# Value matmuls of six groups in f32r high and low parts, in a two-layer attention kernel

## What is computed

```python
def _L0_conv_ref(x, ...):            # layer 0, 64 inner channels
    g_x     = einsum('ic,bcn->bni', g_w, xf) + g_b
    theta_x = einsum('ic,bcn->bni', theta_w, xf) + theta_b
    phi_x   = einsum('ic,bcn->bin', phi_w, xf) + phi_b
    f = softmax(einsum('bni,bim->bnm', theta_x, phi_x), axis=-1)
    y = einsum('bnm,bmi->bni', f, g_x)
    return einsum('ci,bin->bcn', W_w, y.transpose(0, 2, 1)) + W_b + xf

def _L1_conv_ref(x, ...):            # layer 1, 128 channels
    q = einsum('oc,bcn->bno', Wq, xf) + bq
    k = einsum('oc,bcn->bcn', Wk, xf) + bk   # row sums of Wk scale x
    v = einsum('oc,bcn->bno', Wv, xf) + bv
    attn = softmax(einsum('bnc,bcm->bnm', q, k) / sqrt(128), axis=-1)
    return x + einsum('bnm,bmc->bnc', attn, v).transpose(0, 2, 1)
```

## Time and profile before

| | |
|---|---|
| median of 3 runs | 3556.16 us |
| profiled execution, its own time | 3554.52 us |
| its span | 3552.7 us |
| TensorE granted clock, mean | 0.992 |
| busy: TensorE / its weight loads | 98% / 56% |
| busy: DVE / ACT / POOL | 66% / 42% / 70% |
| one block of layer 1, from the second on | 62.1 us |

### The profile page before, as it was taken

The page is one execution under the profiler, slowest core; times in us unless marked ns, Lnnn a source line. Parts: engine busy times, 40 slices in busy tenths (PEclk is TensorE's granted clock), DMA queues, the critical chain, the costliest instruction groups (busy, mean ns, idle before and its releaser), DMA issues.

```text
span 3552.7 us, 45057 instructions
## 1 busy us (share of the span) xinstructions
PE 3476.9 (98%) x12740; PEld 1999.6 (56%) x12740; DVE 2360.3 (66%) x3029; ACT 1494.4 (42%) x2017; POOL 2500.8 (70%) x1142
## 2 busy tenths in 40 slices
PE   7999999999999999999999999999999999999999
PEld 4445466666555446666655455666665544566665
DVE  4555577777655557777765555777776555677775
ACT  4445433333444543333345454333334445333333
POOL 4888666666788866666678886666668888566665
PEclk9999999999999999999999999999999999999999
DMA  1000000000000000000000000000000000000000
GB/s 42 19 12 18 27 10 22 12 21 15 19 17 17 18 23 15 16 18 18 13 19 18 18 16 22 16 15 21 15 19 13 18 18 16 18 13 14 13 7 15
DMA packets 34032, 61.66 MB, mean 17 GB/s; under 512 B 5280, under 2 KB 5920, under 8 KB 33568
## 3 DMA queue, kind: packets, MB, share of 16 engines
q1 hardware_dynamic: 33824, 59.23, 5.5%
HBM read 42.44 MB, written 16.78 MB: 17 GB/s over the span
## 4 chain that ended last, share of the span: by engine, by line
PE 90%; DVE 5%; issue 3%; ACT 1%; POOL 0%; SPq 0%; DVEq 0%; DMA 0%; ACTq 0%
PE acc_out L432 22%; PE acc_out L429 14%; PE rough L385 13%; PE scores L407 9%; PE scores L410 7%; PE scores L412 6%; PE scores L416 6%; PE scores L413 6%; DVE piece_max L730 2%; DVE rparts L757 2%; PE rough L367 2%; PE acc_out L373 1%; PE acc_out L452 1%; PE acc_out L441 1%; PE acc_out L447 1%
## 5 line engine op out<-in xcount | busy, mean ns | idle before, releaser
L271 POOL TENSOR_TENSOR sums<-sums,probs 128x1024 f32<-128x1024 f32 x886 | 2117.8, 2390 | 706.2 <-ACT probs L648 566.0
L730 DVE TENSOR_REDUCE piece_max<-rough 128x1 f32<-128x512 f32 x2024 | 1309.5, 684 | 645.1 <-PE rough L385 644.7
L648 ACT ACTIVATE probs<-probs 128x1024 f32<-128x1024 f32 x512 | 542.0, 1059 | 1220.7 <-DVE probs L747 1218.0
L432 PE MATMUL acc_out<-probs,v_vals 128*128 128x512 f32 x2048 | 963.4, 593 | 0.0
L747 DVE TENSOR_TENSOR probs<-scores,shift_rows 128x1024 f32<-128x1024 f32 x512 | 625.4, 1221 | 462.3 <-PE scores L416 448.6
L655 ACT ACTIVATE probs<-scores 128x1024 f32<-128x1024 f32 x512 | 524.5, 1024 | 692.2 <-PE scores L410 690.3
L429 PE MATMUL acc_out<-probs,g_vals 128*64 128x512 f32 x2048 | 549.7, 617 | 0.0
L432 PEld LDWEIGHTS acc_out<-probs,v_vals 128*128 128x128 f32 x2048 | 384.2, 189 | 285.7 <-issue 247.2
L412 PE MATMUL scores<-qry_a,k_hi 128*128 128x512 f32 x1024 | 532.9, 520 | 0.0
L407 PE MATMUL scores<-qry_a,phi_a 128*128 128x512 f32 x1024 | 449.4, 439 | 0.0
L410 PE MATMUL scores<-qry_b,phi_b 128*128 128x512 f32 x1024 | 404.5, 395 | 0.0
(11 more groups left out here) (86 smaller groups left out, 2117.2 us busy)
## 6 DMA issues: line engine op xcount, KB each, us to landing
x_q<-x SPq DMA_DIRECT2D x32, 256.0 KB, 2.7
x_res<-x SPq DMA_DIRECT2D x32, 256.0 KB, 3.0
mid<-mid_new SPq DMA_DIRECT2D x32, 256.0 KB, 2.2
x_q<-mid SPq DMA_DIRECT2D x32, 256.0 KB, 2.8
x_res<-mid SPq DMA_DIRECT2D x32, 256.0 KB, 3.2
out<-result SPq DMA_DIRECT2D x32, 256.0 KB, 2.3
x_kv<-x SPq DMA_DIRECT2D x24, 256.0 KB, 2.8
probs<-x SPq DMA_DIRECT2D x2, 1024.0 KB, 6.5
```

Source lines behind the costliest of these rows:

```text
L271: eng.tensor_tensor(sums[:, parity], sums[:, parity], probs[:, s % P_BUFS], ALU.add).then_inc(s_plus, 1)
L432: last = mm(acc_out[:, parity], cols(v_vals, tile, KT), p, start=tile == 0, stop=tile == TILES - 1)
L648: nc.scalar.activation(probs[:, s % P_BUFS], probs[:, s % P_BUFS], ACT.Exp, scale=SCALES[1]).then_inc(s_whole, 1)
L730: nc.vector.reduce_max(piece_max[:, t, c:c + 1], src, AX.X).then_inc(s_reduced, 1)
```

## The change

In layer 1, the groups 1, 3, 5, 9, 11 and 13 of each block are "halved": their values and probabilities are each split into an f32r high part and a low part, and the value group is six f32r matmuls (high x high, high x low, low x high, for two tiles) instead of two f32 matmuls. The product of the two low parts is left out. For that

- ACT computes the exponential of such a group twice: first into p_hi (f32r), then in place as before; it also copies half of each value block into v_hi.
- POOL subtracts: p_lo = probs - p_hi (128 x 1024) in step s, ahead of the add of the same group; v_lo = v_vals - v_hi (128 x 256) at s = 14 of layer 0's blocks and in the turn.
- TensorE waits for p_lo and v_lo before such a value group; the other ten groups stay as they were.

```diff
+V_LO_AT = 14
+HALVED = (1, 3, 5, 9, 11, 13)
...
+        v_hi = sb("v_hi", [P, BLOCKS, TPG * KT], F32R)
+        v_lo = sb("v_lo", [P, BLOCKS, TPG * KT], F32R)
+        p_hi = sb("p_hi", [P, 2, GC], F32R)
+        p_lo = sb("p_lo", [P, 2, GC], F32R)
...
+            def halved_values(b, g, nth, parity, s):
+
+                pe.wait_ge(s_p_lo, halved(nth, s))
+                pe.wait_ge(l_v, (b + 1) * BLOCKS)
+                n = HALVED.index(s) % 2
+                for h in range(TPG):
+                    hi = v_hi[:, s // TPG, h * KT:(h + 1) * KT]
+                    lo = v_lo[:, s // TPG, h * KT:(h + 1) * KT]
+                    at = slice(h * QB, (h + 1) * QB)
+                    mm(acc_out[:, parity], hi, p_hi[:, n, at], start=False, stop=False)
+                    mm(acc_out[:, parity], hi, p_lo[:, n, at], start=False, stop=False)
+                    last = mm(acc_out[:, parity], lo, p_hi[:, n, at], start=False, stop=False)
+                last.then_inc(s_used, 1)
...
-                    if s >= LAG:
+                    if s >= LAG and st.layer == 1 and s - LAG in HALVED:
+                        halved_values(st.b, st.g, st.nth, st.parity, s - LAG)
+                    elif s >= LAG:
                         value_group(st.layer, st.g, st.parity, s - LAG)
+                    elif st.prev == 1 and GROUPS + s - LAG in HALVED:
+                        halved_values(st.b if st.layer == 1 else st.b - 1, st.g - 1,
+                                      st.nth - 1, 1 - st.parity, GROUPS + s - LAG)
...
             def take_v(n, c, src):
                 act.wait_ge(p_v, n + 1)
+                copy(v_hi[:, bass.ds(c, 1)] if not isinstance(c, int) else v_hi[:, c:c + 1],
+                     src[:, TPG * KT:].unsqueeze(1))
                 copy(cols(v_vals, c), src).then_inc(h_v, 1)
...
-            def probs_shifted(nth, s):
+            def probs_shifted(g, nth, s):
 
                 act.wait_ge(s_shifted, shifted(nth, s))
+                if s in HALVED:
+                    n = HALVED.index(s)
+                    act.wait_ge(s_used, g * GROUPS + HALVED[n - 2] + 1 + P_BUFS - (GROUPS if n < 2 else 0))
+                    nc.scalar.activation(p_hi[:, n % 2], probs[:, s % P_BUFS], ACT.Exp, scale=SCALES[1])
                 nc.scalar.activation(probs[:, s % P_BUFS], probs[:, s % P_BUFS], ACT.Exp,
                                      scale=SCALES[1]).then_inc(s_whole, 1)
...
+            def split_v(n, c):
+                pool.wait_ge(h_v, n + 1)
+                at = bass.ds(c, 1) if not isinstance(c, int) else slice(c, c + 1)
+                lo_part(v_lo[:, at], cols(v_vals, 2 * c + 1, TPG * KT).unsqueeze(1), v_hi[:, at], l_v)
+
+            def split_probs(g, nth, s):
+                n = HALVED.index(s) % 2
+                pool.wait_ge(s_whole, whole_of(g, s))
+                lo_part(p_lo[:, n], probs[:, s % P_BUFS], p_hi[:, n], s_p_lo)
...
             def block_program(st):
                 for s in range(GROUPS):
+                    if st.layer == 1 and s in HALVED:
+                        split_probs(st.g, st.nth, s)
                     if s < GROUPS - 2 or not st.ends:
                         add(pool, st.layer, st.g, st.parity, s)
...
+                    if s == V_LO_AT and st.kv:
+                        split_v(st.nth - 1, st.i - 1)
```

More of the change, by code:

```diff
@@ L167, in build @@
         s_k_hi = sem("s_k_hi")
-        p_v, h_v = sem("p_v"), sem("h_v")
+        p_v, h_v, l_v = sem("p_v"), sem("h_v"), sem("l_v")
+        s_p_lo = sem("s_p_lo")
         s_settled = {nc.gpsimd: sem("s_settled_pool"), nc.sync: sem("s_settled_sp")}
@@ L272, in add, with halved @@
                               ALU.add).then_inc(s_plus, 1)
+        def halved(nth, s):
+            return nth * len(HALVED) + HALVED.index(s) + 1
         def before(st):
@@ L556, in block_program @@
                     for s in range(GROUPS - LAG, GROUPS):
-                        value_group(st.layer, st.g, st.parity, s)
+                        if st.layer == 1 and s in HALVED:
+                            halved_values(st.b, st.g, st.nth, st.parity, s)
+                        else:
+                            value_group(st.layer, st.g, st.parity, s)
                     if st.turn:
@@ L687, in block_program @@
                     if st.layer == 1:
-                        probs_shifted(st.nth, s)
+                        probs_shifted(st.g, st.nth, s)
                     if s in (DEN_AT + 1, DEN_AT + 2) and st.prev is not None:
@@ L887, in turn @@
                 split_k(nth, BLOCKS - 1)
+                split_v(nth, BLOCKS - 1)
             run_all(pool, turn, block_program)
```

## The result

The changed kernel takes 3496.6 us (median of four runs, 3495.22 to 3498.05), the kernel before 3555.93 in the same comparison. The ratio is 0.9836, with a 95% interval of 0.9823 to 0.9848: 1.6% faster. The forecast was 3495 within 3488 to 3502. The profiled execution took 3498.05 us (span 3496.2), 56.5 less than that of before; the sum had said 61.2.

A forecast was written before the change was run, and what follows sets the result against it. TensorE's instruction stream, busy 98%, was taken as the bound. Savings of 56.4 + 4.2 + 1.05 - 0.5, 61 us, gave 3493.3 for the profiled run, 3495 as median; own range 3488 to 3502, full range 3488 to 3551.

The forecast's parts named there:

- the sum: Whole kernel: 27 steady blocks x (1.56 + 0.53) = 56.4, plus 4.2 and 1.05, less 0.5: 61 us off.
- The value groups: TensorE, layer 1: each halved value group goes from 1.73 to 1.38 us, saving 0.35.
- Which of the six count: Steady layer 1 block: of six short value groups five count, 5 x 0.35 - 0.04 - 0.15 = 1.56 us.
- the third piece of step 12: TensorE's third rough piece in step 12 waits for DVE's reduction, so the short value group's 0.35 us is lost.
- saved TensorE time alone (67 us): 192 short value groups, 0.35 us each: 67 us in all if TensorE alone decides.
- The 0.53 us stop: Step 7, steady layer 1 block: TensorE's second rough piece waits for DVE's reduction; the change gains this 0.53 us.
- margin of 0.11 us: At the reciprocals, DVE reaches line 757 at 16.32 us after group 1's shift starts, 0.11 before POOL's fourth add.
- rival (a): At the reciprocals DVE misses the gap between POOL's adds; steady block gains 0.09 us, total 7, 3549; chance 0.21.
- the subtraction wait for add 4: DVE's second small reciprocal operation (line 759) waits for POOL's fourth add until 18.85, taking about 2.4 us.
- about 46.5: Very last block: POOL's 13 adds, 6 splits and fold take about 46.5 us, making the end 0.5 us longer.
- (b): Rival: some blocks catch DVE's gap at the reciprocals and some miss it, as jitter decides: 3505 to 3540; chance 0.10.
- (c): Rival: POOL becomes the bound if a 1024-wide split costs over 3.4 us; 3726 at 4.8; chance 0.06 with another rival.

The follow-up runs named there:

- run 3: The changed kernel with group 9 not halved (five halved groups): 3495.40 us, ratio to before 0.9831.
- run 4: The changed kernel with the last third rough piece of layer 1 in step 13 instead of 12: 3485.52 us, ratio to before 0.9803.
- run 5: The kernel before, with POOL's low part of the next queries in step 7 instead of 5 in layer 1 blocks: 3546.24 us, ratio 0.9975.
- run 1: The changed kernel with all layer 1 value groups back as two f32 matmuls, splits still made but unused: 3582.32 us, ratio to before 1.0076.
- run 2: The changed kernel without POOL's 192 subtractions, the p_lo matmul using p_hi again: 3491.45 us, ratio to before 0.9820.
- run 8: The changed kernel with the last third piece in step 13 and no group halved in the very last block: 3483.47 us, ratio to before 0.9800.
- run 7: The changed kernel with group 7 halved too and layer 1's third pieces in steps 7, 8, 11, 13: 3487.00 us, ratio to before 0.9809.

## Why the prediction was right

**The value groups.** Six f32r matmuls 0.230 apart, 1.38 us: as in the rows above. TensorE waited for p_lo only in the last block, and for v_lo nowhere.

**Which of the six count.** Group 9 was said to be lost to the third piece of step 12. Runs 3 and 4 show it from both sides: its short form gave nothing, and 11 us came at once when the piece left that step. Counting saved TensorE time alone (67 us) would have been 8 us too much, and is no farther off only because this loss (31 x 0.35 = 11) and the gain below (run 5: 9) nearly cancel.

**The 0.53 us stop.** It went, and run 5 shows that it was what the prediction said. Run 1 shows the other side: the same splits with DVE 0.35 us later cost 27 us. The step of the prediction that gave the sign of this term worked with a margin of 0.11 us between line 757 and add 4. In the block above the cast is issued at 16.26 in that count (575.35 less 559.09, the start of group 1's shift) where 16.32 was worked out, and add 4 starts at 16.55 where 16.43 was. Both errors, 0.06 and 0.12, fell to the safe side, and together they are larger than the margin. Over the 26 steady blocks that passed, the cast starts 0.05 to 0.29 us ahead of add 4. So the mechanism was right, and that it came out on this side was in part luck; the prediction itself gave rival (a) 0.21.

**A detail that was wrong.** I had the subtraction wait for add 4 (2.4 us). In most blocks of the first three images it too slips through, in 0.16; in others it takes 2.27 to 2.36. What decides is which comes first: in the first sort the subtraction starts 0.01 to 0.02 us ahead of add 4, in the second 0.06 to 0.16 behind it. The two sorts of blocks are equally long:

```profile
575.35 0.23 DVE L797 CAST rparts<-rcol 128x4 fp32r<-128x4 f32 x1
635.49 0.17 DVE L797 CAST rparts<-rcol 128x4 fp32r<-128x4 f32 x1
695.42 0.23 DVE L797 CAST rparts<-rcol 128x4 fp32r<-128x4 f32 x1
```

The subtraction behind the middle one took 2.27 us, behind the others 0.16. They are 60.1 and 59.9 us apart, and it is the second stretch that has the long wait in it. So one wait is hidden in DVE's slack and two are not, which is why the cast decides and the subtraction does not.

**The sum, place by place.** From the cast in one image's first steady block to the next image's it is 877.6 us before (515.8 to 1393.4) and 861.3 after (515.42 to 1376.68): 16.4 saved, where the terms give 7 x 2.09 + 1.05 + 0.35 = 16.0; the next two images save 16.7 and 15.2. Layer 0's blocks are as long as before (46.3). The last image saves 7.9 (399.1 to 391.2) where the terms give about 12, and that is 4.1 of the 4.7 us between the sum and the profiled run. Another 1.2 stand ahead of the very first cast (113.69 against 112.46, in layer 0), which the traces of all ten kernels place anywhere from 112.1 to 113.7; the rest nearly cancels. Three places hold the 4.1. Between the second and third cast stands a halt of DVE that the kernel before has too, but here TensorE's clock fell after it (below): 62.1 us against 62.0, nothing saved. Then comes a block of rival (a), the only one among the 27:

```profile
3217.35 1.51 DVE L797 CAST rparts<-rcol 128x4 fp32r<-128x4 f32 x1
3218.89 2.31 DVE L799 TENSOR_TENSOR rparts<-rcol,rparts 128x4 fp32r<-128x4 f32 x1
```

It lasts 59.6 us where its neighbours last 58.2. And the last block was mis-sized. From the shift of its group 1 to the last cast it takes 55.4 us (3432.84 to 3488.23), 1.7 more than before (53.7, 3491.01 to 3544.68), where the terms of the prediction give 0.9 in this count (0.5 with the 0.35 saved ahead of it). The path was right: POOL's row, then DVE's adds and fold. But the row takes 47.2 us where "about 46.5" was put. TensorE's wait for p_lo is not what decides: run 1 makes the same splits and nobody waits for them, and its last block takes 55.2 us in the same count (3517.49 to 3572.70), with DVE's last adds waiting for POOL there too. With five splits (run 3) it is 53.2 (3430.99 to 3484.20). Run 2 prices POOL's splits in the end at 3.6 us, and run 8 prices halving the last block at 1.7 by its trace.

**The rivals.** (a) was a real state of this kernel, one block in 27, and run 1 is it throughout; (b), a mixture, is strictly what happened, though at 1 in 27, and not by jitter: it is the block in which DVE had halted, and the same block has a long cast in runs 3, 4, 7 and 8 too (1.42 to 2.27 us). (c) did not come: a 128x1024 split into f32r took 2.39 us, an add 2.41, as the equal prices at 512 had said. But its mechanism, POOL as the bound, did show in the last block, and POOL's lateness cost TensorE time in run 7.

## What to carry to other kernels

When one engine is full, price a change by where its shorter instruction stands: ahead of a wait that another engine sets, it is worth nothing, and moving the wait by a step (one number of a table) was worth 11 us beside the 59 of the whole change here. Two SBUF operations on 2 KB each can cost microseconds if they come while another engine holds the port; look up in a timeline on which instruction they land before and after the change, since work added to the other engine can move them into a seam as well as out of it. And where a step is repeated 27 times with the same phase, a third of a microsecond in the arrival of one engine (run 1: 27 us) is not noise that averages out but a cliff.

## What the runs showed of the hardware

- A small DVE operation can pass between two POOL instructions that follow each other without a pause: 0.23 us at 575.35 and 0.16 at 575.62, while one add runs from 573.16 for 2.40 us and the next starts at 575.64. The Trainium skill (SBUF — State Buffer, Who interferes with whom) has the one that starts first hold the shared port pair for its whole instruction; the traces agree (2.26 and 2.27 in run 1), and show that a small operation issued up to 0.02 us ahead of the next POOL instruction still passes, while one issued 0.06 behind its start waits for all of it.
- DVE's waiting time is inside its instruction durations, so its busy time fell by 5 us a block with the same instructions. A busy share of such an engine is not its load. ACT shows no such waiting here: its 128x1024 exponentials out of SBUF took 1.04 to 1.07 us each, before and after.
- At the start of a block of the last image (3196.68) DVE had stood 4.56 us with nothing to wait for that the profile shows ("issue"), and TensorE stood behind it until 3198.5. In the stretch 3198 to 3204 (last row) the mean granted clock was 0.72, so TensorE ran part of it at the lower level, 1.2 GHz, and its four value records printed 3.44 us instead of 1.88. The kernel before has a like halt at the same place (4.40, to 3248.66), but its clock stayed at 1.00; TensorE stood idle for 1.02 us there and for 1.56 here. What makes the halt wasn't tried. The DMA view of the changed kernel has two packets of the instruction queue between 3188 and 3197, and none in eight other stretches of 9 or 10 us in layer 1, so DVE may have been waiting for its own code; that isn't shown.

The busy times of that stretch, with the columns of the earlier trace rows:

```profile
3198.00:3204.00 6.00, 5.35 (x11) 2.78 (x12) 3.42 (x5) 2.99 (x3) 1.57 (x1) 0.72 0.00 0
```
